# Two transformer layers, batch by batch: first attention's front steps moved one batch ahead, two heads per 32-row slot, second attention's queries packed and spread by DMA

## The reference

```
# first attention (bfloat16 products, 16 heads of width 8, causal mask and key mask, biases)
q = norm(x) Wq + bq;  k = ctx Wk + bk;  v = ctx Wv + bv
x1 = x + softmax(mask(q k^T / sqrt(8))) v Wo + bo
# first feed-forward: shared part, and 8 routed experts gated by trunc(softmax(top 2))
x2 = x1 + relu(n Ws1)^2 Ws2 + sum_e prob_e relu(n W1_e)^2 W2_e,   n = norm(x1)
# second attention (float32, 16 heads of width 8, an added bias matrix)
x3 = x2 + softmax(q k^T / sqrt(8) + bias) v wo
# second feed-forward: 8 heads of width 128, v and o each from 8 experts, gated by the two best of a sigmoid
c_h = softmax(q_h k_h^T / sqrt(128)) (sum_e gv_he n V_he);   out = x3 + sum_h sum_e go_he c_h O_he
```

## Time and profile before

| | us |
|---|---|
| time, three runs | 1480.44, 1481.13, 1482.63; median 1481.13 |
| profiled execution | 1481.03, its span 1479.2 |
| PE busy | 1404.5 (95%) |
| DVE busy | 1283.9 (87%) |
| ACT busy | 1275.8 (86%) |
| POOL busy | 859.0 (58%) |

### The profile page before, as it was taken

One profiled execution on the slowest core, in us unless ns is written; L12 is line 12 of the kernel. 1 busy time (PEld: TensorE's weight loads), 2 busy tenths in 40 slices (PEclk: granted clock), 3 DMA queues, 4 the chain that ended last, 5 costly groups with the idle time before them and its releaser, 6 DMA issues.

```text
span 1479.2 us, 34876 instructions
## 1 busy us (share of the span) xinstructions
PE 1404.5 (95%) x9748; PEld 963.9 (65%) x9905; DVE 1283.9 (87%) x5266; ACT 1275.8 (86%) x4428; POOL 859.0 (58%) x1345
## 2 busy tenths in 40 slices
PE   4678999999999999999999999999999999999998
PEld 2455666666676666667666666766666676666654
DVE  3677988998998999899899999989999998998886
ACT  3657888899988889998888999888899988889886
POOL 3113656556565656656565565656556565655567
PEclk8689999999999999999999999999999999999999
DMA  4410000000000000000000000000000000000000
GB/s 136 139 56 16 10 14 16 15 15 12 15 11 14 16 15 15 12 15 11 14 16 15 15 13 15 11 14 16 15 15 13 15 11 14 14 15 7 8 3 4
DMA packets 68960, 30.18 MB, mean 20 GB/s; under 512 B 19168, under 2 KB 68768, under 8 KB 68768
## 3 DMA queue, kind: packets, MB, share of 16 engines
q1 hardware_dynamic: 51552, 19.31, 4.9%
q10 hardware_dynamic: 17216, 8.65, 2.1%
HBM read 17.31 MB, written 2.10 MB: 13 GB/s over the span
## 4 chain that ended last, share of the span: by engine, by line
PE 62%; ACT 13%; DVE 11%; POOL 7%; issue 4%; SPq 2%; DMA 1%; POOLq 0%; ACTq 0%; another core or an unknown queue 0%; DVEq 0%
PE psC L309 43%; PE psA L309 7%; PE psB L309 6%; DVE nmA L2240 5%; ACT PTA L1344 3%; ACT PS L1344 3%; POOL accO L3405 3%; DVE PTB L2365 3%; ACT TE L1344 3%; DVE TE L2497 2%; ACT PTB L1344 2%; SPq L3776 2%; PE psA L421 1%; POOL accO L3413 1%; PE psB L553 1%
## 5 line engine op out<-in xcount | busy, mean ns | idle before, releaser
L3405 POOL TENSOR_TENSOR accO<-accO,TE 128x512 f32<-128x512 f32 x192 | 246.3, 1283 | 143.9 <-DVE TE L2497 137.7
L1344 ACT ACTIVATE TE<-psC,gate 128x128 f32<-128x128 f32 x1024 | 300.1, 406 | 17.7 <-PE psC L309 10.4
L1344 ACT ACTIVATE TE<-psC,gateO 128x128 f32<-128x128 f32 x1024 | 292.5, 375 | 24.8 <-PE psC L309 16.2
L2497 DVE SCALAR_TENSOR_TENSOR TE<-psC,gate,TE 128x128 f32<-128x128 f32 x1024 | 284.5, 339 | 29.5 <-PE psC L309 18.4
L2497 DVE SCALAR_TENSOR_TENSOR TE<-psC,gateO,TE 128x128 f32<-128x128 f32 x1024 | 287.1, 341 | 13.2 <-PE psC L309 8.2
L3393 POOL TENSOR_TENSOR TE<-TE 128x256 f32<-128x256 f32 x256 | 192.4, 752 | 164.5 <-DVE TE L2497 160.4
L309 PE MATMUL psC<-Vh,xTh 128*128 128x512 f32 x512 | 263.3, 514 | 2.3 <-ACT PS L1344 1.2
L309 PE MATMUL psC<-Oh,ch 128*128 128x512 f32 x512 | 262.9, 513 | 0.2
L309 PE MATMUL psC<-Oh,cl 128*128 128x512 f32 x512 | 203.0, 396 | 0.0
L309 PE MATMUL psC<-Vh,xTl 128*128 128x512 f32 x512 | 202.5, 396 | 0.0
L309 PE MATMUL psC<-Ol,cb 128*128 128x512 bf16 x452 | 176.2, 390 | 0.0
(11 more groups left out here) (228 smaller groups left out, 3426.7 us busy)
## 6 DMA issues: line engine op xcount, KB each, us to landing
bdB<-Kc SPq DMA_DIRECT2D x384, 16.0 KB
raw<-in_L_ffn_v_w ACTq DMA_DIRECT2D x8, 512.0 KB, 4.5
raw<-in_L_ffn_o_w ACTq DMA_DIRECT2D x8, 512.0 KB, 4.2
x_sb<-in_x SPq DMA_DIRECT2D x32, 64.0 KB, 2.1
ctx_sb<-in_ctx SPq DMA_DIRECT2D x32, 64.0 KB, 2.0
bdA<-Kc SPq DMA_DIRECT2D x128, 8.0 KB
Qb<-Qc SPq DMA_DIRECT2D x128, 8.0 KB
bias_sb<-in_mask_Bx1xSxS_ff SPq DMA_DIRECT2D x32, 64.0 KB, 1.9
```

What stands on the lines that cost most here:

```text
L1344: return A.activation(o, i, func, **kw)
L2497: m = V.scalar_tensor_tensor(TE[:, i, e], psC[:, p, e * P:(e + 1) * P], gates[:, e:e + 1], TE[:, i, e], ALU.mult, ALU.add)
L3405: G.tensor_tensor(accO[:], TE[:, slot(b, H1)] if h == 1 else accO[:], TE[:, slot(b, H1 + h)], ALU.add).then_inc(o_fe, 1)
```

## The change

Five things are changed together.

1. First attention's front steps (`a_ctxt`, `a_keys`, `a_values`, `a_xt`, `a_queries`, with their copies, biases and DMAs) of batch i stand between `a_proj(i - 1)` and `a_x1t(i - 1)`, ahead of the feed-forward part of batch i-1. Their waits on psA change to fit (`a_atT`, `a_ob`); the first scores and the feed-forward part wait instead. The second normalisation gets its own `stA2`, `mvA2`, `rsA2`.
2. Two heads share a slot in both products with the values: the stationary operand is 18 columns of `V0`/`V1`, in which the head has its 9 columns in the first or second half and zeros in the other; heads 4t + j and 4(t + 2) + j are accumulated in the same 18 rows. The result has 256 columns, not 512, and `a_ut`/`b_ut` have two transposes.
3. The queries of second attention are one product with `WqC1`. ScalarE copies it to `Qc1[:, 0]`, VectorE makes the remainder `Qc1[:, 1]`, and three DMAs spread them into `Qs1`.
4. The keys of second attention go by three DMAs to a DRAM tensor `k_rows`, and from there by four to `bdB`.
5. The orders of all engines are written anew, `start()` and `end()` too; on SP the selectors' load goes first.

```diff
+        def two_in_slot(tile):
+            return tile[:, :, 0:NH * (HD + 1)].rearrange("p k (g s) -> p k g s", g=NH // 2)[:, :, :, 0:HD + 1]
+
+        def of_head(tile, n):
+            n = n * 2 * (HD + 1)
+            return tile[:].rearrange("p k x -> p (k x)")[:, n:n + 2 * (HD + 1)]
+
+        def two_heads(ps):
+            return ps.rearrange("p (g s) -> p g s", s=SLOT)[:, :, 0:2 * (HD + 1)].rearrange("p g (k w) -> p k g w", k=2)
+
+        def by_two(ap2):
+            return ap2.rearrange("p (k g) -> p k g", k=2)
+
         psA = ctx.enter_context(nc.psum_tensor("psA", [P, 2, 512], F32))
...
@@ -332,7 +348,7 @@
                     return
                 pe.wait_ge(s_in[b % 2], 32 * (b // 2 + 1))
                 pe.wait_ge(s_const, IDENT)
-                pe.wait_ge(a_hT, b)
+                pe.wait_ge(a_atT, b)
                 T.transpose(psA[:, 1, 0:P], ctx_sb[:, b % 2], ident).then_inc(a_ctr, 1)
...
@@ -353,7 +369,7 @@
                 if b not in BATCHES:
                     return
                 pe.wait_ge(a_ln, 4 * b + 4)
-                pe.wait_ge(a_x2, b)
+                pe.wait_ge(a_ob, b)
                 T.transpose(psA[:, 0, 0:64].bitcast(BF16), xnbA[:], ident_b[:]).then_inc(a_xtr, 1)
...
                     pe.wait_ge(s_kmA, 16 * (b + 1))
                     pe.wait_ge(s_qA, 16 * NJ * (b + 1))
                     pe.wait_ge(a_qb, b + 1)
+                    pe.wait_ge(a_x2, b)
                 elif t == 1:
                     pe.wait_ge(a_vb, b + 1)
+                    pe.wait_ge(a_hT, b)
                 else:
                     pe.wait_ge(a_nm, 4 * b + t - 1)
...
+                for t in (0, 2, 1, 3):
                     pe.wait_ge(a_p, 4 * b + t + 1)
                     for j in range(NJ):
-                        m = mm(psA[SLOT * j:SLOT * j + HD + 1, 0, t * P:(t + 1) * P], Vaug[:, NJ * t + j, :],
-                               PTA[:, t, j, :])
+                        k, r = t // 2, t % 2
+                        m = mm(psA[SLOT * j:SLOT * j + 2 * (HD + 1), 0, r * P:(r + 1) * P], of_head(V0, NJ * t + j),
+                               PTA[:, t, j, :], k == 0, k == 1)
                 m.then_inc(a_pv, 1)
...
-                for t in range(NT):
-                    m = T.transpose(psA[:, 1, t * P:(t + 1) * P], UA[:, t * P:(t + 1) * P], ident)
+                for r in range(2):
+                    m = T.transpose(psA[:, 1, r * P:(r + 1) * P], UA[:, r * P:(r + 1) * P], ident)
                 m.then_inc(a_utr, 1)
...
@@ -440,12 +459,14 @@
                 if b not in BATCHES:
                     return
                 pe.wait_ge(a_ln2, 4 * b + 4)
+                pe.wait_ge(a_vb, min(b + 2, B))
                 T.transpose(psA[:, 1, 0:P], xnA[:], ident).then_inc(a_x1tr, 1)
...
                 pe.wait_ge(a_x1T, b + 1)
+                pe.wait_ge(a_qb, min(b + 2, B))
                 pe.wait_ge(s_ffn0, 80)
...
                 pe.wait_ge(b_xT, b + 1)
-                for t in range(NT):
-                    m = mm(psB[:, 0, t * P:(t + 1) * P], wq1f[:, t * P:(t + 1) * P], xTB[:])
-                m.then_inc(b_q, 1)
+                mm(psB[:, 0, 0:P], WqC1[:], xTB[:]).then_inc(b_q, 1)
...
                 if t == 0:
                     pe.wait_ge(b_qs, b + 1)
+                    pe.wait_ge(s_qB, 16 * 3 * (b + 1))
                 elif t == 1:
                     pe.wait_ge(b_va, b + 1)
                 else:
                     pe.wait_ge(b_nm, 4 * b + t - 1)
-                pe.wait_ge(s_bdB, 16 * NJ * 3 * (b + 1))
+                pe.wait_ge(s_bdB, 16 * NJ * (b + 1))
                 mm(heads_of(psB[:, t % 2, :]), Qs1[:, t, :], bdB[:, t]).then_inc(b_s, 1)
...
-                for t in range(NT):
-                    m = T.transpose(psB[:, 1, t * P:(t + 1) * P], Qh1f[:, t * P:(t + 1) * P], ident)
+                for r in range(2):
+                    m = T.transpose(psB[:, 1, r * P:(r + 1) * P], UB[:, r * P:(r + 1) * P], ident)
                 m.then_inc(b_utr, 1)
...
                 act.wait_ge(s_attn1, 64)
-                act.wait_ge(s_const, SLOTS1)
-                for r in range(3):
-                    A.mul(WqS1[:, :, r * HD:(r + 1) * HD], wq1_raw.rearrange("p (n d) -> p n d", d=HD), SCALE0)
+                A.mul(compact(WqC1), heads_in(wq1_raw), SCALE0)
...
-                copy(Vaug[:, :, 0:HD], Vb2[:].rearrange("p (n d) -> p n d", d=HD)).then_inc(a_va, 1)
+                copy(V0_heads[:, :, :, 0:HD], Vb2[:].rearrange("p (k g d) -> p k g d", k=2, d=HD)).then_inc(a_va, 1)
...
-                copy(UA[:], psA[:, 0, :]).then_inc(a_u, 1)
+                copy(UA[:], psA[:, 0, 0:2 * P]).then_inc(a_u, 1)
...
-                act.wait_ge(s_bdB, 16 * NJ * 3 * b)
+                act.wait_ge(s_rows, 48 * b)
                 copy(Kc1[:, 0], psB[:, 1, 0:P]).then_inc(b_kh, 1)
...
-                act.wait_ge(b_utr, b)
-                copy(Qh1f.bitcast(F32R), psB[:, 0, :]).then_inc(b_qh, 1)
+                act.wait_ge(s_qB, 16 * 3 * b)
+                copy(Qc1[:, 0], psB[:, 0, 0:P]).then_inc(b_qh, 1)
...
                 act.wait_ge(b_pv, b + 1)
-                act.wait_ge(b_qs, b + 1)
-                copy(Qh1f, psB[:, 0, :]).then_inc(b_u, 1)
+                act.wait_ge(b_utr, b)
+                copy(UB[:], psB[:, 0, 0:2 * P]).then_inc(b_u, 1)
...
-                dve.wait_ge(s_cols, 2)
                 dve.wait_ge(b_qh, b + 1)
-                dve.wait_ge(b_s, 4 * b)
-                V.scalar_tensor_tensor(flat(Qs1[:]), Qh1f, less_q[:], psB[:, 0, :], ALU.mult, ALU.add).then_inc(b_qs, 1)
+                dve.wait_ge(s_qB, 16 * 3 * b)
+                V.tensor_tensor(Qc1[:, 1], psB[:, 0, 0:P], f(Qc1[:, 0]), ALU.subtract).then_inc(b_qs, 1)
...
-            def b_keys(b):
-                if b not in BATCHES:
-                    return
+            def b_queries(b):
+                if b not in BATCHES:
+                    return
+                sp.wait_ge(s_const, SLOTS1)
+                sp.wait_ge(b_qh, b + 1)
+                sp.wait_ge(b_s, 4 * b)
+                load(f(Qs1[0:P:NT]), f(Qc1[:, 0]), s_qB)
+                load(f(Qs1[1:P:NT]), f(Qc1[:, 0]), s_qB)
+                sp.wait_ge(b_qs, b + 1)
+                load(f(Qs1[2:P:NT]), f(Qc1[:, 1]), s_qB)
+
+            def no_keys():
                 sp.wait_ge(s_zeroB, 1)
-                sp.wait_ge(b_ks, b + 1)
+                for k in range(2):
+                    load(k_rows[k, :, 3], f(bdB[:, 0, k]), s_noK)
+
+            def b_keys(b, n):
+                if b not in BATCHES:
+                    return
+                k = b % 2
+                if n == 0:
+                    sp.wait_ge(b_ks, b + 1)
+                    sp.wait_ge(s_bdB, 16 * NJ * (b - 1))
+                    for r in range(3):
+                        load(k_rows[k, :, r], f(Kc1[:, r % 2]), s_rows)
+                    return
+                sp.wait_ge(s_noK, 32)
+                sp.wait_ge(s_rows, 48 * (b + 1))
                 sp.wait_ge(b_s, 4 * b)
                 for j in range(NJ):
-
-                    for r in range(3):
-                        load(f(bdB[SLOT * j + HD * r:SLOT * j + HD * (r + 1), :, j, :]),
-                             f(Kc1[SLOT * j:SLOT * (j + 1), r % 2]), s_bdB)
+                    load(f(bdB[SLOT * j:SLOT * (j + 1), :, j, :]),
+                         k_rows[k, HD * j:HD * (j + 1)].rearrange("x r t s -> (x r) t s"), s_bdB)
```

1567 lines of the change are left out of this document (796 added, 771 removed).

## The result

The changed kernel takes 1471.47 us (median of 4 runs, 1470.32 to 1474.04) where the kernel before takes 1481.31 on the same chip: ratio 0.9935, 95% interval [0.9918, 0.9952]. It is faster, by 9.8 us and not by the 28 of the forecast.

The account below looks back on a forecast made before the run. The prediction took TensorE's queue to bound the even stretch: (1.06 - 0.30) x 27.9 = 21.2 us, and 7 us in the fill, gave 1481.0 - 28.2 = 1453 us, with a range of 1436 to 1478.

Parts of the forecast that it names:

- The removed work: On TensorE, fewer query products and fewer a_ut and b_ut transposes take 1.06 us from each period, 29.6 us in all.
- The query wait: Second attention's first score product waits for the packed query loads, between 0 and 0.68 us a period, taken as 0.3.
- rival C: Wider weight loads for the products with the values come onto TensorE's path, 0.49 us per period: 1467 us, chance 0.08.
- the new order priced at nothing: In the even stretch the rewritten order costs 0 to 0.4 us per period, taken as 0 because it moves off-path steps.
- The forecast falls if VectorE or ScalarE becomes what psC waits for: A sign named beforehand: if psC waits for either engine, the forecast is wrong; both were priced at nothing, hidden under TensorE.
- the fill: In the first batches, earlier first-attention loads and fewer key loads gain 7 us, between 14 gained and 6 lost.
- The selectors' early load: At the head of SP's queue it lets the first products start perhaps 3 us sooner.
- SP's slack, 2.6 us: On SP's queue, the key loads end 2.6 us before the query copy, so b_queries' loads behind them cost nothing.
- rival E: SP's queue slips, so key reads are still being issued when the query copy ends: slower, 1492 us, chance 0.13.
- B: Rival: nothing waits, query loads issue and land at the short end, and orders fit: 43.6 us gained, 1437, chance 0.19.
- D: Rival: the query loads eat most of the gain, stall 0.9 us, no gain in the fill: 1477 us, chance 0.12.
- A: The forecast itself, less TensorE work minus a small query wait, plus a gain at the start: 1443 to 1463, chance 0.48.

Follow-up runs that it names:

- e4: The changed kernel with packed queries and two heads per slot both undone, leaving the new orders and the keys by way of DRAM: 1510.7 us, ratio 1.0197.
- e9: The changed kernel with two buffers for Qs1, second attention's scores reading the queries of the batch before: 1462.8 us, ratio 0.9881.
- e2: The changed kernel with only the packed second queries undone, four products and no query loads: 1491.1 us, ratio 1.0065.
- e1: The changed kernel with SP's start list in the order of the kernel before: 1474.5 us, ratio 0.9948.
- e7: The changed kernel with second attention's keys in twelve direct SBUF-to-SBUF loads, not by way of DRAM: 1562.6 us, ratio 1.0544.
- e3: The kernel before with two heads per slot alone: 1469.1 us, ratio 0.9919.
- e11: The kernel before with two heads per slot and second attention's keys by way of DRAM, in the old order: 1468.1 us, ratio 0.9910.
- e5: The changed kernel with two of VectorE's 16-column c_share products moved ahead of the half outputs: 1472.3 us, ratio 0.9938.

## Why the prediction came out too high in gain

**The terms that held.** The removed work (forecast 1.06 us per period, measured 1.19). The query wait held within its bounds, 0 to 0.68, and was taken too small: 0.3 forecast, 0.47 measured. Its loads are issued 0.6 us apart and land after 1.9 us, between and below the forecast's prices, but the cover is 3.66 us and not 3.88. (The forecast's 2.26 us to the third issue is 0.03 more than 0.81 and two issues of 0.71 give, which changes nothing.) The products with 18 columns (0.88 us for 32, as in the earlier trace rows): rival C falls. The Trainium skill's rule behind it ("TensorE: Matmul & The Clock Gate", LDWEIGHTS: time in proportion to the columns) would, by an estimate from its formula, have added 32 x 7.5 ns = 0.24 us to a row of weight loads; the row went from 0.77 to 0.79.

**The step that failed: the new order priced at nothing.** "Bounds for what the new order costs per period ...: 0 to 0.4 us ... I take 0, since what it moves is off the path". e4 measures order and keys at +0.73 us, outside the bounds. In the full change 0.19 us of it is left beside the query wait, since the two packings take most of its waits away again. The bound was drawn from the longest wait that the kernel before shows, and it does not bound what a new order makes. The slots brought -0.68 in this order and only -0.38 in the old one (forecast 0.45). Two steps hold the difference: the one into a_ut, which waits for ScalarE's copy UA, fell by 0.23 us in the new order and by 0.05 in the old, and the one behind a_att grew by 0.15 in the old order and by 0.02 in the new. So "a microsecond leaves the time only if TensorE's queue gets shorter" held in the old order; in the new one the queue waits in pieces of 0.2 to 0.5 us for psC and for ScalarE's copies, and what frees ScalarE counts too. The prediction named the sign itself ("The forecast falls if VectorE or ScalarE becomes what psC waits for"), and it came. Cost in the sum: 0.76 forecast and 0.53 measured make 0.23 x 27.9 = 6.4 us, of it 0.19 us a period from the order and 0.17 from the query wait, less 0.13 of removed work beyond the forecast. With the last batches, where the gain is smaller, it is 21.2 - 13 = 8 us.

**The second step that failed, and the larger one: the fill.** "I take 7 us gained, between 14 gained and 6 lost". It lost 4.3, within the bounds, with the wrong sign. The term named for the loss ("b_queries' loads lie bare there") is there: e9, without that wait, is 4.9 us ahead at batch 4 and 8 us in time. But packed queries with this wait are still 3.7 us ahead of unpacked ones (e2). What was not counted is the order's own cost, 13.0 us at batch 4 in e4: the first scores 4.2 us late, of which SP's order is 0.6 by e1, and batch 1's front steps before batch 0's feed-forward part, 3 us more between 38.37 and 44.41. The selectors' early load did what was said (products at 14.60, not 17.24) and it bought nothing, since the first scores then wait for first attention's loads: a new wait in place of the old one. Cost in the sum: 11 us. How it splits is known only roughly, since each kernel's fill was seen in one execution and the clocks there differ.

**SP's slack, 2.6 us, was 0.6.** It had no price in the forecast and needed none in the even stretch, but it is why rival E was nearer than it seemed: e7 takes 4.1 us more of SP and makes the time 91 us longer. In the fill, E is there in small: SP is 1.1 us late with the query loads of batch 0. TensorE's waits for first attention's loads (bdA and Qb) grew there too, from 2.4 to 12.0 us in the first 160 us, though most of that stands in place of other waits for loads.

**The rivals.** B is refuted: TensorE waits for the query loads in every period. D priced that wait at 0.9 us where 0.47 was measured, but it was right that the fill would gain nothing. A had the sign, the removed work and nearly the query wait, and not the order or the fill. The time lies between A and D, within the range of 1436 to 1478; C's 1467 is the nearest to it, by chance, since its mechanism is refuted. That the time fell into the range at all is in part luck: the order by itself, with the keys' route, costs 29 us (e4).

**What stays open.** In the whole change, 0.19 us a period beside the query wait is spread over several steps, some longer and some shorter than before. The steps into c_trans are not among them (0.39 before, 0.32 after); the largest single growth is behind the first two score products, 0.74 us before and 1.08 after. What the lower clock in the fill cost (0.87 granted from 120 to 160 us, 0.96 before) was not separated. A kernel with the load of the packed queries a batch ahead in truth, and not of the wrong batch as in e9, was not tried; e9's 1463 us is an estimate of what it could reach.

The cheapest part alone is not measurably worse than the whole: e3 and e11 (0.9919 and 0.9910) against after (0.9935). They ran on other chips, and the intervals overlap, so which is the faster is not shown. With 32 batches, the other four edits together bring no gain that can be measured beyond the two heads per slot: after is 0.15 us a period shorter than e3 and 9.8 us behind it at batch 4.

## What to carry to other kernels

A reordering is not free because it moves steps that were off the path: undo the arithmetic savings and time the order by itself before crediting them. Where a load is put between a product and its reader, count the issuing queue's slack to the tenth in the even stretch, and again for each of the first batches, where nothing covers it. Whether a reader waits for a load is told by the distance from the landing to its start (0.09 us here, each time), where the row of idle time showed a quarter of the wait. And measure a period between results well inside the even stretch, not between inputs over a window that touches the fill.

## What the runs showed of the hardware

A VectorE product of 16 columns whose two inputs lie in SBUF lasts 0.18 us alone and up to 1.29 us beside a GpSimd sum. In the kernel after, VectorE and then GpSimd:

```profile
725.59 1.36 DVE L2469 TENSOR_TENSOR best<-best,gsum 128x16 f32<-128x16 f32 x2
```

```profile
725.59 4.18 POOL L3422 TENSOR_TENSOR accO<-accO,TE 128x512 f32<-128x512 f32 x3
```

In the even stretch the product's shortest, median and longest are 159, 176 and 1294 ns, and one GpSimd sum lasts 1287 ns on the mean, so the longest fits a wait for a whole one. In e5, at another place, the longest is 945. The Trainium skill ("SBUF — State Buffer", SBUF: two separate sides) says that the two engines share a pair of ports which one of them holds for a whole instruction, also against a VectorE operation with two SBUF inputs, where the GpSimd operation reads SBUF, as this sum does; the trace agrees.

A load of 64 KB from SBUF to SBUF with 128 rows of 512 bytes takes 0.60 us of SP's queue and lands 1.9 us after its issue (medians of 96); the read back from DRAM takes the same 0.6 and lands after 2.3. Twelve loads of 32 rows took 8.53 us, 0.71 each, and a whole 64 KB tile from an input 0.43 to 0.57. So the queue is paid by the load, at 0.43 to 0.71 us, and seven in place of twelve save 4.1 us of SP.
